# Ten of the 42 effective FFN weights made in ten attention periods, with buffers and a bank of their own

## The reference, cut to what matters

```
x = x + tanh(g_xattn) * attention(layernorm(x), ctx)          # 32 query heads, 8 key/value heads of 128
x = x + tanh(g_ffn)   * ffn(layernorm(x))

def linear(x, w, su, sv):  return x @ (w * (su @ sv)).T       # su, sv of rank 4
ffn(x) = linear(silu(linear(x, gate)) * linear(x, up), down)  # 512 -> 1792 -> 512
```

## Time and profile before

| | us |
|---|---|
| median of three runs | 1370.74 |
| the profiled execution | 1370.94 |
| its span in the trace | 1369.1 |
| TensorE busy | 1356.6 (99%) |
| VectorE, GpSimd, ScalarE busy | 959.8, 954.4, 561.1 |

### The profile page before, as it was taken

How to read it: one execution, slowest core, us unless ns; L and a number is a source line. 1 busy time by engine, 2 the same in 40 slices (tenths; PEclk the granted TensorE clock), 3 DMA queues, 4 the chain that set the end, 5 groups by cost and what they waited for, 6 DMA issues and landing times.

```text
span 1369.1 us, 21420 instructions
## 1 busy us (share of the span) xinstructions
PE 1356.6 (99%) x7770; PEld 1112.6 (81%) x7770; DVE 959.8 (70%) x1465; ACT 561.1 (41%) x950; POOL 954.4 (70%) x883
## 2 busy tenths in 40 slices
PE   8999999999999999999999999999999999999998
PEld 8988788888888878778787877788888888888887
DVE  6388677665565677666667877774789888766776
ACT  5455555555444523232223334232344434334333
POOL 5599989999887946445454666573787787666664
PEclk9999999999999999999999999999999999999999
DMA  8386787777978866454445556621322331311121
GB/s 294 123 264 220 238 265 237 270 250 234 335 256 294 283 232 224 154 165 129 153 162 150 185 154 200 200 65 45 78 56 68 92 85 47 123 54 47 47 69 70
DMA packets 158057, 226.47 MB, mean 165 GB/s; under 512 B 43264, under 2 KB 89600, under 8 KB 155904
## 3 DMA queue, kind: packets, MB, share of 16 engines
q1 hardware_dynamic: 157952, 225.09, 51.0%
HBM read 155.32 MB, written 69.73 MB: 164 GB/s over the span
## 4 chain that ended last, share of the span: by engine, by line
PE 83%; POOL 10%; DVE 2%; issue 2%; ACT 1%; DMA 1%; SPq 0%; DVEq 0%; ACTq 0%; POOLq 0%
PE bank L616 65%; POOL wa_lo L1676 5%; PE bank L888 4%; PE bank L890 4%; PE bank L766 4%; PE bank L889 4%; PE bank L742 3%; POOL ws L1664 1%; POOL ws L1667 1%; POOL ws L1665 1%; POOL ws L1669 1%; DVE xc L1274 1%; PE bank L659 0%; DMA er_raw<-in_sf_r 0%; POOL xb L1645 0%
## 5 line engine op out<-in xcount | busy, mean ns | idle before, releaser
L616 PE MATMUL bank<-xc,wa_hi 128*128 128x512 f32 x896 | 277.7, 391 | 0.8 <-ACT s L1012 0.8
L616 PE MATMUL bank<-wd_hi,o_hi 128*128 128x512 f32 x512 | 202.9, 396 | 0.5 <-issue 0.5
L616 PE MATMUL bank<-wd_lo,o_hi 128*128 128x512 f32 x512 | 199.5, 390 | 0.0
L616 PE MATMUL bank<-wd_hi,o_lo 128*128 128x512 f32 x512 | 199.2, 389 | 0.0
L616 PEld LDWEIGHTS bank<-xc,wa_hi 128*128 128x128 f32 x896 | 167.3, 188 | 38.1 <-ACT s L1012 2.5
L616 PE MATMUL bank<-xc,wa_lo 128*128 128x512 f32 x448 | 174.5, 390 | 0.0
L1063 ACT ACTIVATE o_hi<-bank 128x512 fp32r<-128x512 f32 x128 | 69.5, 595 | 228.3 <-PE bank L766 151.1
L1477 DVE SCALAR_TENSOR_TENSOR X<-bank,tg,X 128x512 f32<-128x512 f32 x221 | 154.4, 741 | 0.0
L616 PE MATMUL bank<-x_hi,wf_hi 128*128 128x512 f32 x392 | 152.6, 389 | 0.1
L616 PE MATMUL bank<-x_hi,wf_lo 128*128 128x512 f32 x392 | 152.5, 389 | 0.0
L616 PE MATMUL bank<-x_lo,wf_hi 128*128 128x512 f32 x364 | 141.6, 389 | 0.0
(11 more groups left out here) (175 smaller groups left out, 3157.0 us busy)
## 6 DMA issues: line engine op xcount, KB each, us to landing
q_scratch<-q_st SPq DMA_DIRECT2D x32, 1024.0 KB, 4.8
q_sb<-q_scratch SPq DMA_DIRECT2D x64, 512.0 KB, 4.8
w_raw<-in_wq SPq DMA_DIRECT2D x32, 512.0 KB, 4.1
wd_raw<-in_wd SPq DMA_DIRECT2D x16, 1024.0 KB, 4.8
f_raw<-ffn_eff_scratch SPq DMA_DIRECT2D x28, 512.0 KB, 3.7
er_raw<-in_sf_r SPq DMA_DIRECT2D x42, 256.0 KB, 4.3
e_raw<-in_wf SPq DMA_DIRECT2D x42, 256.0 KB, 5.4
ffn_eff_scratch<-e_eff SPq DMA_DIRECT2D x42, 256.0 KB, 5.2
```

The lines of the kernel that those rows point to most:

```text
L616: last = pe.matmul(to, a, b, start=(start and n == 0), stop=(stop and n == 3 * len(pairs) - 1), skip_group_check=onto)
```

## The change

Effective weights 0 to 31 are made in quads 12 to 43, as before, with set 0 of the buffers. Quads 0 to 11, ten of which made one each, make none: no `load_lr`, `load_e`, `lr_hi`, `lr_lo`, matmul, multiply or `store_e` is left there, but for the loads and `lr` parts that run ahead of quad 12. Weights 32 to 41 are made in periods 4 to 13 (`E_LATE`), with set 1 of el_raw, er_raw, e_raw, e_eff, er and el, in memory that the quads' q_st used, and in bank 2, the bank of the weighted values (bank 7 before).

In such a period p: ScalarE's `lr_hi` comes behind `out_hi(u-3)`; VectorE's `lr_lo` behind `out_lo(u-3)`, its multiply behind `add_to_x(2u-7)`; TensorE's matmul ahead of `output(2u-6)`; and TensorE's next weighted values, which write bank 2, wait for the multiply (`v_e`). SyncE loads for p+1 within period p, and stores e_eff of period p-1 in period p, behind `load_wd` where there is one. GpSimd's wait on `v_lr` ahead of its second set of sums is gone.

```
+    E_AT = {q: q - Q0 for q in range(Q0, NQ)}
+    NE = len(E_AT)
+    E_LATE = {4 + n: NE + n for n in range(NP - NE)}
+    def e_bank(m):
+        return bank[2] if m >= NE else bank[7]
...
@@ SyncE, period p
             if p % 2 == 1 and p // 2 + 1 < NWD:
                 load_wd(p // 2 + 1)
+            if p - 1 in E_LATE:
+                store_e(E_LATE[p - 1])
+            if p + 1 in E_LATE:
+                if p + 1 == min(E_LATE):
+                    for n in range(2):
+                        sp.wait_ge(d_qo[n], 16 * NB * NHP // 2)
+                load_lr(E_LATE[p + 1])
+                load_e(E_LATE[p + 1])
...
@@ TensorE, weighted_values(u)
+            elif u % 2 == 0 and u // 2 + 1 in E_LATE:
+                pe.wait_ge(v_e, E_LATE[u // 2 + 1] + 1)
@@ TensorE, period p
             output(2 * u - 7)
+            if p in E_LATE:
+                pe.wait_ge(v_o, 2 * u - 4)
+                effective(E_LATE[p])
             output(2 * u - 6)
...
@@ VectorE, period p
             out_lo(u - 3)
+            if p in E_LATE:
+                lr_lo(E_LATE[p])
             add_to_x(2 * u - 8)
...
             add_to_x(2 * u - 7)
+            if p in E_LATE:
+                effective(E_LATE[p])
@@ ScalarE, period p
             out_hi(u - 3)
+            if p in E_LATE:
+                lr_hi(E_LATE[p])
...
@@ GpSimd, left_sums(w)
-            if w == 1:
-                g.wait_ge(v_lr, 2 * E_MOVE)
```

More of the change, by code:

```diff
@@ L129, in flamingo @@
     t2 = at(199, "t2", [P, BT])
[L130 to L135, removed]
+    er_raw = [at(205, "er_raw0", [P, D]), at(183, "er_raw1", [P, D])]
+    el_raw = [at(207, "el_raw0", [P, P]), at(187.5, "el_raw1", [P, P])]
+    e_raw = [at(161, "e_raw0", [P, D]), at(185, "e_raw1", [P, D])]
+    e_eff = [at(19, "e_eff0", [P, D]), at(179, "e_eff1", [P, D])]
+    er = [at(21, "er0", [P, D], F32R), at(181, "er1", [P, D], F32R)]
+    el = [at(2, "el0", [P, P], F32R), at(187, "el1", [P, P], F32R)]
     q_sb = [at(3, "q_sb0", [P, 2, CB, 2, S]), at(7, "q_sb1", [P, 2, CB, 2, S])]
@@ L403, in load_lr @@
                 sp.wait_ge(v_lr, 2 * m)
[L404 to L408, removed]
+            sp.dma_start(el_raw[m >= NE][:, :], sf_l[m]).then_inc(d_lr, 16)
+            sp.dma_start(er_raw[m >= NE][:, :], sf_r[m]).then_inc(d_lr, 16)
         def load_e(m):
@@ L412, in load_e @@
                 sp.wait_ge(v_e, m)
-            if m == E_MOVE:
+            else:
                 sp.wait_ge(p_p[3], NV)
-            sp.dma_start(e_raw[m >= E_MOVE][:, :], wf[m]).then_inc(d_e, 16)
+            sp.dma_start(e_raw[m >= NE][:, :], wf[m]).then_inc(d_e, 16)
         def store_e(m):
             sp.wait_ge(v_e, m + 1)
-            sp.dma_start(ed[m], e_eff[:, :]).then_inc(d_eo, 16)
+            sp.dma_start(ed[m], e_eff[m >= NE][:, :]).then_inc(d_eo, 16)
         def store_q(q):
@@ L658, in effective @@
                 pe.wait_ge(v_e, m)
-            pe.matmul(bank[7][:, :], el[:96, :], er[:96, :], start=True, stop=True).then_inc(p_e, 1)
+            pe.matmul(e_bank(m)[:, :], el[m >= NE][:96, :], er[m >= NE][:96, :], start=True, stop=True).then_inc(p_e, 1)
         pe.wait_ge(v_ident, 1)
@@ L1048, in output_hi @@
                     a.wait_ge(p_p[3], NQ)
-                    a.wait_ge(v_e, NP)
+                    a.wait_ge(v_e, NE)
             a.activation(wd_hi[k % 2][:, e, :], wd_raw[:, e, :], ACT.Copy).then_inc(a_wd, 1)
@@ L1286, in effective @@
                 v.wait_ge(d_eo, 16 * m)
-            v.tensor_tensor(e_eff[:, :], bank[7][:, :], e_raw[m >= E_MOVE][:, :], ALU.mult).then_inc(v_e, 1)
+            n = m >= NE
+            v.tensor_tensor(e_eff[n][:, :], e_bank(m)[:, :], e_raw[n][:, :], ALU.mult).then_inc(v_e, 1)
         def quad(q):
@@ L1377, in out_lo @@
             if u == 3:
-                v.wait_ge(d_eo, 16 * NP)
+                v.wait_ge(d_eo, 16 * NE)
             for n in range(2):
```

34 lines of the change are left out of this document (13 added, 21 removed).

## The result

| | before | after |
|---|---|---|
| median of six runs each, us | 1370.43 (1368.88 to 1371.98) | 1375.23 (1374.51 to 1379.79) |
| the profiled execution | 1370.94 | 1374.51 |
| its span | 1369.1 | 1372.7 |

The ratio of after to before is 1.0045, 95% interval 1.0034 to 1.0055: the change makes the kernel slower by nearly half a per cent. The prediction was 1372.8, range 1369.0 to 1377.0. The median lies inside the range, and outside the forecast's own range of 1371 to 1374.5. It lies 0.2 us under what rival B would give (1375.4 to 1377.9).

What follows compares the result with a forecast made beforehand. TensorE was taken as the bound, busy for 1356.6 of 1369.1 us. From the profiled 1370.94, less 1.7 for early quads, plus 3.3 for odd and 0.3 for even periods, came 1372.8 us, range 1369.0 to 1377.0.

Steps and rivals of the forecast that it cites:

- rival B: Odd periods: the store lands 5.8 to 6.3 us after issue, stall 1.17 to 1.67 each, 1375.4 to 1377.9 us; chance 0.23.
- What only moves: TensorE: ten matmuls of 0.23 us leave the quads and ten enter the attention, net 0.
- Quad 4: TensorE's wait for VectorE's t goes with the er subtraction ahead of it: 0.7 us gained.
- Quad 10: TensorE's wait for ScalarE's kq shrinks as GpSimd's chain comes forward: 0.6 us gained, bounds 0 and 1.0.
- Quad 13: TensorE's wait for s goes because er_raw's load is 1.05 us earlier without a store ahead: 0.4 us gained.
- Odd periods: Periods 5 to 13: weighted values wait for e_eff, held by the store behind load_wd: 0.67 us each, 3.3 in all.
- the three stores: Profiled e_eff stores right behind a 1 MB DMA, landing after 5.1 to 5.3 us, taken for the odd periods' store.
- Even periods: The er subtraction, slowed beside GpSimd, just fits its matmul's slot: 0.06 us a period, 0.3 in five.
- Loads: nothing: Loads for the next period are issued about a period ahead of their use and cost nothing.
- A: Odd periods: the store lands in time, leaving only the gains and the even periods' cost: 1369.5 us; chance 0.17.
- C: Even periods: er passes behind both of GpSimd's wd_lo operations, 6.0 us in place of 0.3: 1378.5 us; chance 0.04.
- D: Early quads: GpSimd's own pace holds quads 10 and 13, gains only 0.7 us: 1373.8 us; chance 0.06.

Runs made afterwards that it cites:

- e7: The changed kernel plus the engine work of ten effective weights back in quads 0 to 6 and 9 to 11, reading weight 0's pair, loaded once: 1379.08 us.
- e8: e7 plus ten 256 KB stores of the repeated products where the early quads' stores stood, one in quad 12: 1379.38 us.
- e12: The changed kernel with the five wd_raw loads of periods 5 to 13 bringing half their 1 MB: 1368.12 us.
- e9: The changed kernel with only the first of ten late weights loading e_raw, the other nine reusing that tile: 1375.00 us.
- e10: The changed kernel with only the first of ten late weights loading el_raw and er_raw, the others reusing that pair: 1374.93 us.

## Why the prediction was right or wrong, point by point

- **What only moves.** Right: 2.3 us left the quads. In the periods the slot costs 0.25 where I had 0.23, 0.2 us over ten.
- **Quad 4.** Right in its mechanism; 0.99 us in the traces over the whole quad where I had 0.7. I had left out a second, smaller delay of 0.13 right behind, that went with it, and 0.15 in quad 12.
- **Quad 10.** Right: 0.47 of the 0.99 went, for 0.6 forecast, and e7 brings it back by VectorE's and ScalarE's work alone. The chain through the statistics is what I argued; the runs show that engine work and not DMAs drives it, not each of its links.
- **Quad 13.** The step failed. "The load is 1.05 us earlier": it is, but what was late in quad 12 was a landing after 5.14 us, and e8, with the store back, has no wait there. The 0.4 belonged to the execution that I read. The same holds for quads 21 and 25, of which I said that they stay: they come and go with quad 13, without any doing of the change.
- **Odd periods.** The place and mechanism are right: five waits of the weighted values for e_eff, which waits for the store; issue at 8.5 and 8.9 us into the period, as forecast. The size was off. The step that failed is "I choose near the three stores, because their queue is the most like this one": the store took 5.5 to 5.8 us, 5.6 in the mean, for 5.3. By the prediction's own sign (after 5.5) this is rival B, its mean 0.2 us under B's lower bound. e12 shows that the landing moves with the bytes ahead. But my three had the same 1 MB ahead of them, a q store that landed after 4.4 to 4.8, so equal bytes were not enough to make the rows alike; why the store takes 0.3 us more behind this load stays open.
- **The handovers there.** 0.08 us was wrong: from landing to VectorE 0.12, and from VectorE's end to TensorE's first matmul 0.26, 0.3 us more in each odd period and 1.5 in five. With the 0.3 of the landing that is about the whole step from 0.67 to 1.26 us a period. The rows had it: quads 4, 10 and 13 each lost 0.16 more than they were idle, and I used that for the quads and not here.
- **Even periods.** The pair of subtractions came out as forecast, 0.63 and 1.67 us. The matmul came 0.08 us later than due for 0.06, and lost as much again in the restart: with it the period lost 0.18, 0.9 in five for 0.3.
- **Loads: nothing.** Right in effect, by e9 and e10.
- **Rivals.** A fell (no store under 5.5 us in an odd period). C fell: er let one GpSimd operation pass. D fell in its reason: quads 4 and 10 gave back 1.5. B came nearest, in its sign and in the time.
- **The sum.** Gains of the change 1.6 (forecast 1.7, near it by luck: 0.4 of the 1.7 was never the change's, and as much stood uncounted in quads 4 and 12); odd periods 5 x 1.26 = 6.3 (3.3), even ones 0.9 (0.3), slots 0.2: 5.8 us over before, for 1.9 forecast. The medians differ by 4.8, and the ratio's interval gives 4.7 to 7.5. The time lies in the stated range because the range was drawn to hold most of B. The first profile of before had 2.0 us in quads 13, 21 and 25 which the profile of after had not, and 0.7 at the start, and after had 0.4 near 357 us; so the two spans, 3.6 apart, hide part of the cost (3.6 + 2.0 + 0.7 - 0.4 = 5.9), and those of after and of before's second profile, 7.1 apart, overstate it.

## What to carry to other kernels

A buffer that is written again only after its store has landed puts that store on the critical path; look at what stands ahead of it in the DMA queue, in bytes, and either move it ahead of the large transfer or give it a second buffer: both took away here the 1.1 to 1.4 us a period that waiting cost, at no price. To the idle time of a new wait add the restart, 0.1 to 0.3 us here, each time. And before small waits of one profile are counted as a gain, ask for a second execution of the same program: of the 4.0 us that the first two traces gave for the quads, 2.0 went with one late landing and 0.7 lay at the program's start.

## What the runs showed of the hardware

- Two DMAs on one queue share more than an order: 256 KB issued 0.37 us behind 1 MB made that 1 MB land 0.5 us later (4.7 to 4.8 alone, 5.2 to 5.4 so), and landed themselves 0.7 us behind it.
- With 512 KB in place of 1 MB ahead, the same store landed 1.3 to 1.6 us sooner.
- A load of 256 KB, in the same place of the same program, landed after 5.14 us in one execution and 3.73 in another.
- After a wait TensorE's first matmul came 0.26 us behind the end of VectorE's operation that released it, and VectorE 0.12 us behind a DMA's landing.
- TensorE rose to its 2.4 GHz level 2 us earlier in one execution of the kernel before than in another (9.12 and 11.27 us), worth 0.9 us to the whole: 256 columns took 0.21 us ahead of the rise and 0.12 behind it.
- TensorE's granted clock fell to 0.50 in a wait of 4.01 us, and the matmuls up to its rise lost 2.9 us on top of the wait.
